# Sums, statistics, Relu and casts between the products with the counts: by halves before, by blocks or partly earlier after

## What is computed

```python
# network 0: two layers of this; mean and variance are over the 3125 nodes, per channel
agg = segment_sum(x[src], dst)
h = ((1 + eps) * x + agg) @ w_a + b_a
h = (h - h.mean(axis=0)) * rsqrt(h.var(axis=0) + 1e-5) * g + bt
h = relu(h) @ w_b + b_b                      # relu behind layer 0, none behind layer 1
# networks 1 and 2: messages over the edges with gathered rows (most of the time), not touched
# network 3: twice
x = relu(segment_sum(x[src], dst) @ W.T + b)
```

## Time and profile before

| | us |
|---|---|
| median of 3 runs | 3587.89 (3583.38 to 3591.75) |
| the profiled execution | 3585.43 |
| its span in the trace | 3584.1 |
| TensorE busy, share of the span | 2579.5, 72% |
| VectorE busy | 1998.7, 56% |
| ScalarE busy | 1526.7, 43% |
| GpSimd busy | 2009.4, 56% |
| granted TensorE clock, mean over the span | 0.823 |

### The profile page before, as it was taken

How to read it: one execution, slowest core, us unless ns; L and a number is a source line. 1 busy time by engine, 2 the same in 40 slices (tenths; PEclk the granted TensorE clock), 3 DMA queues, 4 the chain that set the end, 5 groups by cost and what they waited for, 6 DMA issues and landing times.

```text
span 3584.1 us, 57380 instructions
## 1 busy us (share of the span) xinstructions
PE 2579.5 (72%) x12616; PEld 1659.6 (46%) x12616; DVE 1998.7 (56%) x3057; ACT 1526.7 (43%) x3452; POOL 2009.4 (56%) x1999
## 2 busy tenths in 40 slices
PE   4887976766667565666986565569965556599898
PEld 1334445555555344444654343446644444366444
DVE  8886764444445444446964444459844444588211
ACT  8674443333334333334743333337633333367211
POOL 0000007777763777776747777768667777677000
PEclk7999987677878777668996877769987777799999
DMA  2002026555544878875968887849678888578200
GB/s 72 0 1 115 1 67 201 162 169 163 168 114 140 263 262 262 261 261 170 327 214 261 262 263 260 263 136 319 240 255 260 264 263 263 181 276 287 116 1 18
DMA packets 271543, 679.40 MB, mean 190 GB/s; under 512 B 48513, under 2 KB 81206, under 8 KB 270038
## 3 DMA queue, kind: packets, MB, share of 16 engines
q1 hardware_dynamic: 156758, 336.25, 28.4%
q0 software_dynamic: 73216, 190.95, 18.4%
q10 hardware_dynamic: 41472, 151.01, 11.1%
HBM read 502.07 MB, written 175.94 MB: 189 GB/s over the span
## 4 chain that ended last, share of the span: by engine, by line
POOL 36%; PE 32%; issue 16%; DMA 6%; DVE 5%; ACT 3%; DVEq 2%; POOLq 1%; ACTq 0%; SPq 0%
POOL region L414 19%; POOL tN L414 17%; PE psum L490 9%; PE psum L741 9%; PE psum L504 5%; DMA region<-tab,idx_ring 3%; PE psum L706 2%; PE psum L580 2%; PE psum L721 2%; DMA tN<-tab,idx_ring 1%; DVE acc L1453 1%; DVEq L1088 1%; ACT psum L1809 1%; DMA region<-tabs,idx_ring 1%; DVE region L1092 1%
## 5 line engine op out<-in xcount | busy, mean ns | idle before, releaser
L934 PE MATMUL psum<-w_all,region 128*128 128x256 f32 x2496 | 913.7, 534 | 632.6 <-ACT region L1795 611.6
L934 PEld LDWEIGHTS psum<-w_all,region 128*128 128x128 f32 x2496 | 642.9, 269 | 903.0 <-issue 714.0
L414 POOL DMA_INDIRECT region<-tab,idx_ring x624 | 591.5, 948 | 319.3 <-issue 314.4
L414 POOL DMA_INDIRECT tN<-tab,idx_ring x624 | 590.1, 946 | 190.2 <-issue 182.2
L414 POOL DMA_INDIRECT region<-tabs,idx_ring x208 | 206.7, 994 | 588.6 <-issue 586.7
L1942 POOL TENSOR_TENSOR region<-node_no,dst_rel 128x256 f32<-128x256 f32 x312 | 413.6, 1326 | 137.4 <-ACT region L1839 112.6
L1461 DVE TENSOR_TENSOR tN<-tN,psum 128x1024 f32<-128x1024 f32 x156 | 190.5, 1221 | 417.8 <-DMA tN<-tab,idx_ring 409.5
L1453 DVE TENSOR_TENSOR acc<-acc,psum 128x1024 f32<-128x1024 f32 x312 | 379.1, 1215 | 46.2 <-ACT psum L1809 46.1
L1461 DVE TENSOR_TENSOR region<-region,psum 128x1024 f32<-128x1024 f32 x156 | 190.4, 1220 | 377.9 <-DMA region<-tab,idx_ring 356.0
L1809 ACT ACTIVATE psum<-region 128x1024 f32<-128x1024 f32 x156 | 160.2, 1027 | 439.5 <-DVE acc L1453 280.5
L1809 ACT ACTIVATE psum<-tN 128x1024 f32<-128x1024 f32 x156 | 160.2, 1027 | 402.9 <-DVE acc L1453 402.9
(11 more groups left out here) (310 smaller groups left out, 3470.9 us busy)
## 6 DMA issues: line engine op xcount, KB each, us to landing
region<-e_t SPq DMA_DIRECT2D x416, 256.0 KB
pre_dram<-region ACTq DMA_DIRECT2D x144, 512.0 KB, 3.6
pre_dram<-tN ACTq DMA_DIRECT2D x144, 512.0 KB, 3.9
region<-pre_dram SPq DMA_DIRECT2D x144, 512.0 KB, 5.0
tN<-pre_dram SPq DMA_DIRECT2D x144, 512.0 KB, 5.0
tA<-dst_row SPq DMA_DIRECT2D x78, 256.0 KB
adj_kept<-region SPq DMA_DIRECT2D x5, 2000.0 KB, 16.9
region<-adj_kept SPq DMA_DIRECT2D x5, 2000.0 KB, 17.0
```

The lines of the kernel that those rows point to most:

```text
L414: pool.indirect_dma_start(m_ring[j][:, c, at:at + width], None, table[:, :], bass.IndirectOffsetOnAxis(ap=idx_at(j, k)[:, c:c + 1], axis=0 ...
L934: mm = pe.matmul(banks[:, 2 * (j % 2) + c // 2, (c % 2) * 256:(c % 2) * 256 + 256], e_ring[:, j % E_SLOTS, c * D:(c + 1) * D], W(f"ee{l}") ...
```

## The change

What changes, with the lines of the kernel before:

1. `gin` adds `(1 + eps) * x` by seven blocks, and the first product waits for each block instead of each half.
2. Sum and squares go: ScalarE only empties the banks, VectorE takes `BN_STATS` of each block of `a1` as it comes out, and one `BN_AGGR` gives mean and variance. ScalarE takes the root of that. A one-column root is put ahead of the first product on ScalarE, and the table load stands there.
3. The Relu goes by seven blocks, and the second product waits for each.
4. `turn_tA` deals its turns as `adadddd`: ScalarE empties quads 0 and 2, VectorE the other five. ScalarE casts the first half of part 0 when quads 0 to 2 are out, the second when all are.
5. In the `degrees` form of `norm_blocks` ScalarE casts the first half as soon as quads 0 to 3 are scaled, before it scales quads 4 to 6.
6. `dense()` waits at its first matmul also for all turns on ScalarE and VectorE, since it writes all PSUM banks.

```diff
-        ALTERNATE = "adadada"
+        CAST_BETWEEN = "adadddd"
...
+                        pe.wait_ge(S["turn_act"], T["turn_act"])
+                        pe.wait_ge(S["turn_dve"], T["turn_dve"])
...
             def gin(layer, inT, g_, bt):
                 c = chan
-                for h in BLOCK_HALVES:
-                    dve.scalar_tensor_tensor(out=a0[:, h], in0=inT[:, h], scalar=one_eps[:, layer:layer + 1], in1=a0[:, h],
+                for a, b in blocks():
+                    dve.scalar_tensor_tensor(out=a0[:, a:b], in0=inT[:, a:b], scalar=one_eps[:, layer:layer + 1], in1=a0[:, a:b],
                                              op0=ALU.mult, op1=ALU.add).then_inc(S["gin_in"], 1)
-                turns = T.turns("a" * N_BLOCKS)
-                wait_turns(dve, turns)
-                dve.wait_ge(v.sem, v.did(dve.tensor_reduce(c[:, 0:1], node_sums, AX.X, ALU.add)))
-                dve.tensor_scalar(c[:, 1:2], c[:, 0:1], -1.0 / N_NODES, None, ALU.mult).then_inc(S["gin_mean"], 1)
...
+                for n, (k, (a, b)) in enumerate(zip(T.turns("a" * N_BLOCKS), blocks())):
+                    dve.wait_ge(S["turn_act"], k.out[1])
+                    v.did(dve.bn_stats(out=node_stats[:, 6 * n:6 * n + 6], in_=a1[:, a:min(b, N_NODES)]))
+                dve.wait_ge(v.sem, v.n)
+                dve.bn_aggr(out=c[:, 0:2], in_=node_stats).then_inc(S["gin_var"], 1)
...
             def gin(ba, bb, func):
                 c = chan
-                act_product(act, T.turns("a" * N_BLOCKS), a1, ACT.Identity, col(ba), node_sums)
...
-                act.activation(a0[:, 0:N_NODES], a1[:, 0:N_NODES], ACT.Square, bias=c[:, 1:2], accum_out=c[:, 2:3]
-                               ).then_inc(S["act_done"], 1)
...
-                for h in BLOCK_HALVES:
-                    act.activation(a0[:, h], a1[:, h], ACT.Relu, bias=c[:, 6:7], scale=c[:, 5:6]).then_inc(S["gin_hid"], 1)
+                act.activation(c[:, 7:8], eps_c[:, 0:1], ACT.Sqrt)
+                act_product(act, T.turns("a" * N_BLOCKS), a1, ACT.Identity, col(ba))
+                act.wait_ge(S["gin_var"], T["gin_var"] + 1)
+                act.activation(c[:, 3:4], c[:, 1:2], ACT.Sqrt, bias=eps_c[:, 0:1]).then_inc(S["act_done"], 1)
                 act.wait_ge(S["gin_coef"], T["gin_coef"] + 1)
+                for a, b in blocks():
+                    act.activation(a0[:, a:b], a1[:, a:b], ACT.Relu, bias=c[:, 6:7], scale=c[:, 5:6]).then_inc(S["gin_hid"], 1)
...
                 act_empty(act, turns, to_nodes, quads())
+                wait_turns(act, turns[0:3])
+                cast_first(y3, 0)
                 wait_turns(act, turns)
...
+                cast_first(y3, 1)
+
+            def cast_first(src3, n):
+                act.copy(parts[0][:, HALVES[n], :], src3[:, HALVES[n], :]).then_inc(S["part_cast"], 1)
...
+                    if cast and step == N_BLOCKS + 1:
+
+                        act.wait_ge(S["nrm_cent"], T["nrm_cent"] + 3)
+                        cast_first(xN[:, :, :], 0)
```

69 lines of the change are left out of this document (27 added, 42 removed).

## The result

The changed kernel took 3565.19 us, median of 5 runs (3563.26 to 3566.18); the kernel before, run twice more beside it, 3583.38 (five runs, 3576.54 to 3591.75). The ratio is 0.9947, 95% interval 0.9937 to 0.9958: 19.0 us less, from 15.1 to 22.6. I had said 3573, a gain of 14.9 on the 3587.89 then known. So of the 7.8 us between forecast and result, 4.5 lie in the level of the kernel before (3587.89 against 3583.38) and 3.3 in the gain (18.2 between the medians against 14.9). The direction was right, and the time lies 0.8 us under the range. In the pair of profiles the span went from 3584.1 to 3563.8 us, TensorE's mean granted clock from 0.823 to 0.824.

A forecast was written before the change was run, and what follows sets the result against it. It took a chain of waits between engines, one working at a time in layer 0's `gin`, as the bound. 7.8 + 0.7 + 3.1 + 2.8 = 14.4 us off 3585.43 gave 3571.0, 3573.5 on the median, said as 3573; range 3566 to 3580.

The forecast's parts named there:

- The median of the three is 2.5 higher: Whole kernel before: median 3587.89 against the profiled 3585.43, which moved the forecast from 3571.0 to 3573.5.
- Behind 520 us the loops of networks 1 and 2 are untouched: Gather loops of networks 1 and 2: same length as before, only beginning 11.6 us earlier.
- the gain doesn't show: Rival, whole kernel: the gain is lost in the gathers or the spread of runs, 3583 us, chance 9%.
- Start of `gin`: Layer 0: TensorE starts after VectorE's first 512-column block instead of the first half, 1.09 us gained.
- Clock: Layer 0, first product of `gin`: shorter idle time keeps TensorE at full clock, 1.66 us gained.
- Emptying and statistics: `gin`, layer 0: dropping padding pieces and sums gives 0.25 us, `BN_STATS` and `BN_AGGR` statistics 3.85 us.
- the dear rival: Rival, both layers: `BN_STATS` takes 1.36 us a block, 4.4 us less gain, 3578 us, chance 12%.
- Relu: `gin`, layer 0: the second product waits for one Relu block instead of the first half, 0.98 us gained.
- the turns: `turn_tA`, layer 0: redealt copies and earlier cast let `dense()` start sooner, 0.7 us taken, from nothing to 0.9.
- Layer 1: Layer 1: TensorE goes on 3.3 us earlier after the fold products, less 0.2 for half clock, 3.1 us gained.
- Network 3: Before `dense()` in network 3: the jump into the `Else` loads code and hides the whole gain, 0 us.
- that rival: Rival, network 3: the jump isn't last, 1.8 + 2.1 = 3.9 us more gain, 3569 us, chance 12%.

The follow-up runs named there:

- e5: The changed kernel run again, unedited, beside the kernel before: 3568.41 us, ratio 0.9945.
- e9: The kernel before with six VectorE memsets ahead of network 1's first `pass_ready`, a delay of 14.3 us: 3591.62 us, ratio 1.0031.
- e14: The kernel before with the same six memsets as e9, profiled again: 3594.94 us in one run, beside 3580.90.
- e8: The changed kernel with the sum at the head of `gin` in two pieces instead of seven blocks: 3576.21 us, ratio 0.9963.
- e12: The changed kernel without the early one-column root on ScalarE: two runs, 3565.01 us (profiled) and 3819.73 us, only the profile read.
- e11: The changed kernel with the Relu of `gin` in two pieces, as in the kernel before: 3566.76 us, ratio 0.9963.
- e4: The changed kernel with six VectorE memsets ahead of network 1's first `pass_ready`, a delay of 14.3 us: ratio 0.9966.
- the first set: The runs e1 to e4, with slower gathers: the kernel before took 4422.13 us there, median of 36 runs.
- e15: The changed kernel run a third time, unedited, beside the kernel before: 3569.14 us, ratio 0.9965.
- e1: The kernel before, run again without any change: ratio 0.9996.
- e2: The changed kernel with parts 4 and 5 undone, so turns and casts as in the kernel before: ratio 0.9969.
- e6: The changed kernel with the Relu of `gin` in three pieces instead of seven: 3571.02 us, ratio 0.9946.
- e16: The changed kernel with the Relu of `gin` in three pieces, as in e6, run again: 3566.45 us, ratio 0.9959.

## Why the prediction was right, and where it was wrong

**The gain.** Three pairs (the record has chip 6 for the second, 5 for the third and none for the first) gave 0.9947, 0.9945 and 0.9965, 19.0, 19.7 and 12.5 us. The table gives, from the means of four profiles before and three after, 31.10 - 22.95 = 8.1 in layer 0, 44.3 - 39.5 = 4.8 in layer 1, 3.0 behind network 2, 0.2 lost in network 3: 15.7 us, which lies within the intervals of all three pairs. E adds 0.6 by e5 alone, in which the clock didn't fall. The loops, with 4.5 added in e9 and e14 for what the stores hide, are 2790.5 on average in the four profiles before, 2788.0 in the three after and 2791.2 in all ten profiles that have the changed code around them: no difference that holds. My 14.4 is 1.3 short of 15.7. The rest of the first pair's 19.0 is not explained by the change; in its profiles it lies in the loops.

**The step that failed** is the last one of the sum, from the stretches to the time of the whole, with the width of the range. The gain was sized well; two assumptions under the level were not. "The median of the three is 2.5 higher" took 3587.89 for the level of the kernel before; five runs gave 3583.38, 4.5 lower, and runs of it lie 9 to 21 us apart in the four sets in which its median is 3581 to 3588. From 3583.38 the same gain of 14.9 gives 3568.5, inside the range. And "Behind 520 us the loops of networks 1 and 2 are untouched" was true of the code but not of the time, for which the sum put nothing: they took 2787.8 where 2792.3 had been, and 2786.6 to 2799.1 us over the profiles of the table (e9 and e14 with 4.5 added). The low end, 3566, gave only 3 us to all this. The rival "the gain doesn't show" had the spread of runs in it, but only towards a lost gain; the same spread made it larger. One of the prediction's own signs of being wrong came: the loops took another time than before. What makes them vary stays open.

**Step by step.** Start of `gin`, 1.09: measured 1.07. Clock, 1.66: 7.30 to 5.61, 1.69; it fell in the first product in every profile with 2.83 to 2.91 us of idle time ahead (e8 too) and in none with 1.76 or 1.77. Emptying and statistics, 4.10: from TensorE's end to the Relu 2.96 now (355.22 - 352.26), 6.92 before, 3.96. The terms that I gave for the statistics add up to 354.94 and not to 354.99 as I wrote, so 4.15 was meant. `BN_STATS` at 0.69 against 0.68 taken, the aggregate 0.34 against 0.4; the dear rival is out. Relu, 0.98: 0.86 at the product's start, since the first block takes 0.81 and not 0.7 (e12), and half of that, 0.47 by e11, at `dense()`. "The second product keeps its 7.92" was wrong: 8.29 to 8.67, or 7.02 when it starts late (e8), and what starts it sooner is worth half. So the parts don't add up in layer 0: 7.58 at the start of the product, 7.2 at its end; the turns, 0.7, gave 0.94, and the total 8.15 against my 8.5 came out near partly by luck, by two errors that cancel. Layer 1, 3.1: 3.4 against the short form; the 0.2 for half clock wasn't needed, ScalarE's late emptying cost 0.2 instead, and against the long form it is 6.1, which no row that I had shows. Behind network 2, 2.8: 3.0. Network 3, 0: in the changed kernel's three profiles nothing on average, as said; where the packet comes early, up to 1.9 and 1.7 more for the clock (3.9 had been given to that rival). The packet of the earlier trace rows moved 0.5 us or so behind the end of the last transpose (3453.54), not "just when the transposes were issued", which changes nothing in the reading. The table load "without that cover would cost its 1.28": 0.16 at the Relu (e12).

**Not settled**: why the loops of the same code differ by 12 us, why e4's were 16 or more shorter in the first set, why that set is slow, whether the change or chance keeps the clock up in layer 1's first product, and whether e5's 19.7 and e15's 12.5 differ by more than chance.

## What to carry to other kernels

Read a stretch in two or three profiles of the same kernel before pricing it: here one of them hid a 2.7 us loss that another showed, in a place that seemed settled. Where the clock has fallen, ask when it comes back: here that moment did not move with the start, and work brought forward into the half clock gave half of the time by which it came earlier (0.47 of 0.92, 1.31 of 2.61). And where untouched loops make up nearly four fifths of the time, their spread, not the sum of the terms, sets the width of the range.

## What the hardware did that I had not expected

- The clock fell to 1.2 GHz for some 3 us around the start of layer 1's first product in e1, e2, e9 and e14, and not in the others, behind the same pauses of 1.15 and 0.25 us.
- In the changed kernel's layer 1 an idle time of 2.87 us left the next product at full clock (2.81 us in e5, 3.09 in e6); the same idle time was followed by a half clock within that product in e8 and e16 (4.51 and 4.57 us).
- A jump whose code has to be loaded started TensorE's next work 1.29 to 3.20 us behind its last, by the moment at which one packet moved.
- Just behind the start of network 3's second product the clock fell in nine of the ten profiles with 2.09 us or more of idle time ahead, and in none of the four with at most 1.92; the fall cost 1.7 us.
